# Attention's values times probabilities as three split products, with the transposes in the scores' banks amid the output projection

## The chip, the cores and the metric

The kernel runs on one core of a Trainium2 chip. The metric is the device time of one execution in microseconds; the kernel before takes 1842.34 us, median of three runs (1841.61 to 1843.49). Engines: PE is TensorE (PEld its weight loads), DVE is VectorE, ACT is ScalarE, POOL is GpSimd, SP issues the transfers.

## The reference, cut to what matters

Four layers with a norm and a residual around each: a state-space layer, a gated MLP with integer weights, attention, and a second gated MLP. The input is 4 batches x 256 tokens x 512, all float32. The change lies in attention, which has 32 query heads in 8 groups; each group shares one key and one value head of 128:

```
q = q * cos + rotate_half(q) * sin
scores = einsum('bhqd,bhkd->bhqk', q, k) * scale          # causal mask
attn = softmax(scores)
out  = einsum('bhqk,bhkd->bhqd', attn, v)                 # the product that is changed
return out.reshape(b, 256, 4096) @ Wo.T                   # output projection
```

## The kernel before

The attention phase (`attention_mlp_phase`) works in 32 units, one for each group g (8) and batch b (4), v = 4g + b. A unit has 4 query heads and 256 queries in two halves of 128 (QT = 2). Because of the causal mask the first 128 queries need only the first 128 keys; so a unit has three blocks of transposed probabilities, 128 keys x 512 (4 heads x 128 queries): first half, second half on keys 0, second half on keys 1.

Most matmuls are split: each operand is written as a high part (rounded to float32r by ScalarE) and a low part (the rest, by VectorE or GpSimd), and high x high, high x low and low x high are added. The scores and the product of values and probabilities are plain float32 matmuls; the profile shows such a matmul as two (x2).

PSUM has eight banks of 512 float32 columns: 0 and 1 hold the queries' product (`ps_q`), 2 to 4 the scores (`s0`, `s1`), 5 to 7 are `X[0]`, `X[1]`, `X[2]`. Before the change the three transposes go to `X[2]`, `X[0]`, `X[1]`, are copied to SBUF as `pt`, and the products of values go to `X[2]` and `X[0]`; the output projection of a unit also goes to `X[0]` (t=0) and `X[1]` (t=1).

Each engine has its own queue, written out by hand in a `body(g, b)`, and semaphores order them. TensorE's body for unit v is: `queries` of v+1 (48 split matmuls, L1355); `output` of v-1 (24 split matmuls, L1380 to L1382); `attend` of v (12 transposes, L1389 and L1394, and the float32 products, L1398 to L1402); `scores` of v+1 (L1366, L1368). Meanwhile the next query is made ready: ScalarE's `turn` (L1491, L1492) copies it with its halves exchanged, GpSimd's `sine` (L1631) multiplies that in SBUF, VectorE's `cosine` (L1703) multiplies the unturned one out of PSUM, and `rotate` (L1710) adds the two in SBUF. After the scores VectorE adds the mask and takes maxima (L1715 to L1722), ScalarE takes exponentials (L1500, L1503), and VectorE multiplies by the inverse sums (`probabilities`, L1728 to L1733).

Weights: in b=2 ScalarE splits the next group's query weights and GpSimd makes their low part (L1635); in b=0 the same is done for the output weights (L1515, L1639). `accumulate` (L1739) adds the output projection to `acc` on VectorE.

VectorE's queue before, in one unit:

```
values(v)                  # copy V to vs, L1804
cosine(v + 1)
accumulate(v - 1)          # t = 0, 1; waits for the output projection
copy X[0] to pt            # L1816
rotate(v + 1)
ol = X - oh, t = 0, 1      # L1823
maxima(v + 1); probabilities(v + 1)
```

Of the kernel before, what the change touches and what calls it, by code (L numbers as in the profile page):

```python
# [1237 lines left out]
def attention_mlp_phase(nc, M, place, raw, wqh, wql, K, V, acc, wq, wo, w_mlp, b_mlp, hidden, down, mid,  # L1238
# [12 lines left out]
    flipped, p_kept_act, p_kept_dve, v_here, summed, o_hi, o_lo, o_prod, added = (  # L1251
        sem("flipped"), sem("p_kept_act"), sem("p_kept_dve"), sem("v_here"), sem("summed"), sem("o_hi"), sem("o_lo"),
# [16 lines left out]
    q = place("q", [P, HPG, SEQ])  # L1269
    direct, turned = place("direct", [P, HPG * SEQ]), place("turned", [P, HPG * SEQ])  # L1270
    pa, pb = place("pa", [P, HPG, P]), place("pb", [P, HPG, SEQ])
    pt = place("pt", [P, 3, HALF])
    oh, ol = place("oh", [P, QT, HALF], F32R), place("ol", [P, QT, HALF], F32R)
    vs = place("vs", [P, QT, HD])
# [6 lines left out]
    X = [M.ps[:, 5 + i, :] for i in range(3)]  # L1281
    ps_t = [M.ps[:, i % 2, :] for i in range(TT)]
# [30 lines left out]
    with nc.Block() as block:  # L1313
# [30 lines left out]
        def _(pe):  # L1344
# [26 lines left out]
            def output(g, b):  # L1371
                v = g * BATCH + b
                if b == 0:
                    pe.wait_ge(wo_hi, g + 1)
                    pe.wait_ge(wo_lo, g + 1)
                pe.wait_ge(o_lo, v * 2 + 2)
                for t in range(QT):
                    for h in range(HPG):
                        part = slice(h * P, (h + 1) * P)
                        nc.tensor.matmul(X[t], oh[:, t, part], woh[:, h, :], start=(h == 0), stop=False)  # L1380
                        nc.tensor.matmul(X[t], oh[:, t, part], wol[:, h, :], start=False, stop=False)  # L1381
                        mm = nc.tensor.matmul(X[t], ol[:, t, part], woh[:, h, :], start=False, stop=(h == HPG - 1))  # L1382
                    mm.then_inc(o_prod, 1)

            def attend(g, b):
                v = g * BATCH + b
                pe.wait_ge(normed, v + 1)
                for h in range(HPG):
                    mm = nc.tensor.transpose(X[2][:, h * P:(h + 1) * P], pa[:, h, :], ident)  # L1389
                mm.then_inc(flipped, 1)  # L1390
                for i in range(QT):
                    at_least(pe, added, v * 2 - 1 + i)
                    for h in range(HPG):
                        mm = nc.tensor.transpose(X[i][:, h * P:(h + 1) * P], pb[:, h, i * P:(i + 1) * P], ident)  # L1394
                    mm.then_inc(flipped, 1)
                pe.wait_ge(v_here, v + 1)
                pe.wait_ge(p_kept_act, v * 2 + 1)
                nc.tensor.matmul(X[2], vs[:, 0, :], pt[:, 0, :], start=True, stop=True).then_inc(summed, 1)  # L1398
                pe.wait_ge(p_kept_dve, v + 1)
                nc.tensor.matmul(X[0], vs[:, 0, :], pt[:, 1, :], start=True, stop=False)  # L1400
                pe.wait_ge(p_kept_act, v * 2 + 2)
                nc.tensor.matmul(X[0], vs[:, 1, :], pt[:, 2, :], start=False, stop=True).then_inc(summed, 1)  # L1402
# [37 lines left out]
            def body(g, b):  # L1440
                if more(g, b):
                    queries(*after(g, b))
                if b > 0:
                    output(g, b - 1)
                elif not (isinstance(g, int) and g == 0):
                    output(g - 1, BATCH - 1)
# [9 lines left out]
            output(GROUPS - 1, BATCH - 1)  # L1456
# [29 lines left out]
        def _(act):  # L1486
# [70 lines left out]
            def body(g, b):  # L1557
# [12 lines left out]
                act.wait_ge(flipped, v * 3 + 1)  # L1570
# [7 lines left out]
                for t, x in ((0, X[2]), (1, X[0])):  # L1578
                    act.wait_ge(summed, v * 2 + t + 1)
                    nc.scalar.activation(oh[:, t, :], x, ACT.Copy).then_inc(o_hi, 1)  # L1580
# [498 lines left out]
```

## Time and profile before

| | |
|---|---|
| median of three runs | 1842.34 us (1841.61 to 1843.49) |
| the profiled execution | 1840.51 us |
| its span, first to last instruction | 1838.7 us |
| mean granted TensorE clock | 0.971 of full speed |
| TensorE busy | 1676.4 us, 91% of the span, 8214 matmuls |
| VectorE / ScalarE / GpSimd busy | 1097.3 / 869.0 / 822.2 us |
| HBM traffic | 54 GB/s over the span |

The profile is of one execution. A row of the timeline is one instruction, or several alike after each other (xN): start, duration, engine, line of the kernel, operation, output and input. A matmul's duration is longer than the distance to the next, since they are pipelined; the distance from start to start is what a matmul costs. In brackets stands how long the engine had been idle and what ended that. The attention units run from about 951 us to 1572 us of the span.

### The profile page before, as it was taken

How to read it: one execution, taken by the hardware profiler on the slowest of the kernel's cores; microseconds unless marked ns; L12 is line 12 of the kernel's file. 1: busy time of each engine (PE TensorE's matmuls, PEld its weight loads, DVE VectorE, ACT ScalarE, POOL GpSimd, SP SyncE). 2: the span in 40 equal slices, each digit the busy share in tenths (PEclk: the TensorE clock that was granted, in tenths of full speed). 3: DMA queues.
4: the chain of work that ended last, by engine and by line, in shares of the span. 5: the costliest groups of instructions: out<-in, count | busy, mean ns of one | idle time of the engine just before them, and what ended most of it. 6: DMA issues, size and time to landing. Idle time of an engine off the chain costs nothing. (4 is left out here: it accounts for less than half of the span.)

```text
span 1838.7 us, 24233 instructions
## 1 busy us (share of the span) xinstructions
PE 1676.4 (91%) x8214; PEld 1376.5 (75%) x8214; DVE 1097.3 (60%) x1592; ACT 869.0 (47%) x1761; POOL 822.2 (45%) x416
## 2 busy tenths in 40 slices
PE   5994999999998799898989999999999998799988
PEld 4851788888886688676877778787788786778777
DVE  4326999999995332452915666666666767622232
ACT  2336777777763353333624445454444545433231
POOL 2200999999984362342512232222222323365353
PEclk9997999999999899998999999999999999999989
DMA  3101100011100394001100010000100010144100
GB/s 113 63 1 72 47 35 35 36 34 35 34 0 24 134 355 163 18 1 57 63 23 24 24 47 23 23 23 23 46 23 23 23 58 35 70 142 160 42 18 29
DMA packets 25188, 100.84 MB, mean 55 GB/s; under 512 B 3104, under 2 KB 3360, under 8 KB 22560
## 3 DMA queue, kind: packets, MB, share of 16 engines
q1 hardware_dynamic: 24976, 99.89, 15.1%
q8 instruction: 40, 0.66, 0.1%
q14 instruction: 28, 0.23, 0.0%
q10 hardware_dynamic: 144, 0.07, 0.0%
HBM read 97.72 MB, written 2.23 MB: 54 GB/s over the span
## 5 line engine op out<-in xcount | busy, mean ns | idle before, releaser
L1001 PE MATMUL psum<-scratch_s,res_const 128*128 128x256 f32 x1024 | 250.4, 383 | 4.7 <-DVE scratch_s L960 4.0
L1631 POOL TENSOR_TENSOR stretch_turned<-stretch_turned,res_const 128x1024 f32<-128x1024 f32 x32 | 80.3, 2509 | 386.6 <-ACT stretch_turned L1492 386.6
L1001 PEld LDWEIGHTS psum<-scratch_s,res_const 128*128 128x128 f32 x1024 | 191.8, 190 | 43.0 <-DVE scratch_s L960 18.3
L858 POOL TENSOR_TENSOR scratch_s<-scratch_s,scan_cm 128x1024 f32<-128x1024 f32 x64 | 150.9, 2358 | 27.6 <-DVE scratch_s L944 27.6
L944 DVE TENSOR_TENSOR_SCAN scratch_s<-psum,scratch_s 128x512 f32<-128x512 f32 x128 | 153.4, 1198 | 8.5 <-ACT psum L899 8.5
L1355 PE MATMUL psum<-opnd_xh,query_wqh 128*128 128x256 f32 x512 | 151.5, 296 | 1.9 <-PEq L94 1.9
L846 POOL TENSOR_TENSOR scratch_s<-scan_bm,scratch_s 128x1024 f32<-128x1024 f32 x64 | 150.9, 2359 | 0.1
L1355 PE MATMUL psum<-opnd_xh,query_wql 128*128 128x256 f32 x512 | 145.6, 284 | 0.0
L1355 PE MATMUL psum<-opnd_xl,query_wqh 128*128 128x256 f32 x512 | 145.5, 284 | 0.0
L1500 ACT ACTIVATE stretch_pa<-psum,stretch_nm 128x128 f32<-128x128 f32 x128 | 45.2, 365 | 197.0 <-DVE stretch_nm L1722 197.0
L995 PE MATMUL psum<-scan_diag,scratch_s 128*128 128x256 f32 x512 | 132.9, 383 | 0.5 <-ACT scratch_s L891 0.5
L899 ACT ACTIVATE psum<-ssm_dt,ssm_vec 128x255 f32 (+1 forms) x256 | 110.8, 465 | 11.8 <-DVE scratch_s L944 11.3
L995 PEld LDWEIGHTS psum<-scan_diag,scratch_s 128*128 128x128 f32 x512 | 95.9, 193 | 13.0 <-ACT scratch_s L891 0.9
L1355 PEld LDWEIGHTS psum<-opnd_xh,query_wqh 128*128 128x128 f32 x512 | 99.0, 193 | 3.2 <-issue 2.3
L1380 PE MATMUL psum<-stretch_woh,stretch_oh 128*128 128x512 f32 x256 | 100.3, 392 | 0.5 <-DVE stretch_ol L1823 0.5
L1381 PE MATMUL psum<-stretch_wol,stretch_oh 128*128 128x512 f32 x256 | 100.0, 390 | 0.0
L1382 PE MATMUL psum<-stretch_woh,stretch_ol 128*128 128x512 f32 x256 | 99.9, 390 | 0.0
L1355 PEld LDWEIGHTS psum<-opnd_xl,query_wqh 128*128 128x128 f32 x512 | 98.9, 193 | 0.8
L1355 PEld LDWEIGHTS psum<-opnd_xh,query_wql 128*128 128x128 f32 x512 | 98.7, 193 | 0.0
L235 PE MATMUL psum<-stretch_wh,stretch_hh 128*128 128x512 f32 x176 | 71.1, 404 | 17.2 <-ACT stretch_wh L284 15.5
L960 DVE TENSOR_TENSOR scratch_s<-psum,scan_cm 128x512 f32<-128x512 f32 x128 | 85.2, 665 | 0.0
L950 DVE TENSOR_TENSOR_SCAN psum<-scan_decay,psum 128x512 f32<-128x512 f32 x64 | 78.1, 1221 | 0.0
(269 smaller groups left out, 4322.4 us busy)
## 6 DMA issues: line engine op xcount, KB each, us to landing
mi_dw<-in_dw SPq DMA_DIRECT2D x24, 448.0 KB, 5.7
mi_dm<-in_dm SPq DMA_DIRECT2D x24, 448.0 KB, 6.4
query_raw<-in_w_q SPq DMA_DIRECT2D x8, 1024.0 KB, 4.7
query_raw<-in_w_o SPq DMA_DIRECT2D x8, 1024.0 KB, 4.8
scan_cm<-bc_rows SPq DMA_DIRECT2D x12, 512.0 KB, 4.1
gu_raw<-in_w_gu SPq DMA_DIRECT2D x11, 512.0 KB, 8.0
mlpa_raw<-in_w_mlp SPq DMA_DIRECT2D x7, 768.0 KB, 4.3
mlpa_base<-in_b_mlp SPq DMA_DIRECT2D x7, 768.0 KB, 5.8
```

What stands on the lines that cost most here:

```text
L846: nc.gpsimd.tensor_tensor(by_state(shared[r][h]), bm[:, 4 * h:4 * h + 4, :], u[r].rearrange("p (a t) -> p a t", a=1).broadcast_to((P, 4, S ...
L858: nc.gpsimd.tensor_tensor(shared[r][h], shared[r][h], weights(4 * h, 4), ALU.mult).then_inc(weighted_pool, 1)
L899: ins = nc.scalar.activation(by_state(bank)[:, n, 1:SEQ], flat_dt[:, bass.ds(s * SEQ + 1, SEQ - 1)], ACT.Exp, scale=M.vec[:, bass.ds(s * N ...
L944: nc.vector.tensor_tensor_scan(quarter(r, i), decay_shared[i % 2], quarter(r, i), 0.0, ALU.mult, ALU.add).then_inc(scanned, 1)
L960: nc.vector.tensor_tensor(own[i], state[i], weights(NH + 2 * i, 2), ALU.mult).then_inc(weighted, 1)
L995: mm = nc.tensor.matmul(by_state(state[i])[:, :, t * P:(t + 1) * P], ut[r][:, t * P:(t + 1) * P], diag[:, t, 2 * i:2 * i + 2, :], start=Tr ...
L1001: mm = nc.tensor.matmul(ps_y[r], ident, part[:, n * SEQ:(n + 1) * SEQ], start=False, stop=stop and (n + 1) * SEQ == part.shape[1])
L1355: mm = nc.tensor.matmul(ps_q[:, h * SEQ:(h + 1) * SEQ], w[:, k, h * HD:(h + 1) * HD], x[:, k, b * SEQ:(b + 1) * SEQ], start=(k == 0 and w ...
L1380: nc.tensor.matmul(X[t], oh[:, t, part], woh[:, h, :], start=(h == 0), stop=False)
L1381: nc.tensor.matmul(X[t], oh[:, t, part], wol[:, h, :], start=False, stop=False)
L1382: mm = nc.tensor.matmul(X[t], ol[:, t, part], woh[:, h, :], start=False, stop=(h == HPG - 1))
L1631: nc.gpsimd.tensor_tensor(heads(turned[:, :]), heads(turned[:, :]), over_heads(C_SIN, SEQ), ALU.mult).then_inc(q_sine, 1)
```

## The change

The product of values and probabilities is split like the others. ScalarE writes `vh` (rounded values) and `ph` (rounded probabilities, all three blocks) and VectorE writes `vl` and `pl`, the rests. Nine float32r matmuls take the place of three float32 ones. The transposes go to `turned_p`, banks 2 to 4 of the scores, and stand on TensorE between the first half of the heads of the t=1 output projection of the unit before and its second half (in the last unit after all of it). The projection's input `oh`, `ol` of t=0 shares its memory with `ph`, `pl` block 0; `direct` and `q` share one buffer, and `rotate` works in place. VectorE accumulates t=0 before, t=1 after the subtractions and `rotate`. The start of the diff renames semaphores accordingly.

```diff
@@ -1266,12 +1266,13 @@
     woh, wol = place("woh", [P, HPG, DM], F32R), place("wol", [P, HPG, DM], F32R)
-    q = place("q", [P, HPG, SEQ])
-    direct, turned = place("direct", [P, HPG * SEQ]), place("turned", [P, HPG * SEQ])
+    q, turned = place("q", [P, HPG, SEQ]), place("turned", [P, HPG * SEQ])
+    direct = q[:, :, :].rearrange("p a c -> p (a c)")
     pa, pb = place("pa", [P, HPG, P]), place("pb", [P, HPG, SEQ])
-    pt = place("pt", [P, 3, HALF])
-    oh, ol = place("oh", [P, QT, HALF], F32R), place("ol", [P, QT, HALF], F32R)
-    vs = place("vs", [P, QT, HD])
+    ph, pl = place("ph", [P, 3, HALF], F32R), place("pl", [P, 3, HALF], F32R)
+    o_last = [place(n, [P, HALF], F32R) for n in ("oh", "ol")]
+    oh, ol = (ph[:, 0, :], o_last[0][:, :]), (pl[:, 0, :], o_last[1][:, :])
+    vh, vl = place("vh", [P, QT, HD], F32R), place("vl", [P, QT, HD], F32R)
     mx, nm, sums, inv = (place(n, [P, 8]) for n in ("mx", "nm", "sums", "inv"))
...
@@ -1279,6 +1280,7 @@
     X = [M.ps[:, 5 + i, :] for i in range(3)]
+    turned_p = [M.ps[:, 2 + i, :] for i in range(3)]
     ps_t = [M.ps[:, i % 2, :] for i in range(TT)]
...
@@ -1368,38 +1370,50 @@
 
-            def output(g, b):
+            def output(g, b, t, first=0, end=HPG):
                 v = g * BATCH + b
-                if b == 0:
-                    pe.wait_ge(wo_hi, g + 1)
-                    pe.wait_ge(wo_lo, g + 1)
-                pe.wait_ge(o_lo, v * 2 + 2)
-                for t in range(QT):
-                    for h in range(HPG):
-                        part = slice(h * P, (h + 1) * P)
-                        nc.tensor.matmul(X[t], oh[:, t, part], woh[:, h, :], start=(h == 0), stop=False)
-                        nc.tensor.matmul(X[t], oh[:, t, part], wol[:, h, :], start=False, stop=False)
-                        mm = nc.tensor.matmul(X[t], ol[:, t, part], woh[:, h, :], start=False, stop=(h == HPG - 1))
+                if first == 0 and t == 0:
+                    if b == 0:
+                        pe.wait_ge(wo_hi, g + 1)
+                        pe.wait_ge(wo_lo, g + 1)
+                    pe.wait_ge(o_lo, v * 2 + 2)
+                if first == 0:
+                    at_least(pe, added, v * 2 - 1 + t)
+                for h in range(first, end):
+                    part = slice(h * P, (h + 1) * P)
+                    nc.tensor.matmul(X[t], oh[t][:, part], woh[:, h, :], start=(h == 0), stop=False)
+                    nc.tensor.matmul(X[t], oh[t][:, part], wol[:, h, :], start=False, stop=False)
+                    mm = nc.tensor.matmul(X[t], ol[t][:, part], woh[:, h, :], start=False, stop=(h == HPG - 1))
+                if end == HPG:
                     mm.then_inc(o_prod, 1)
 
-            def attend(g, b):
+            def flips(g, b):
                 v = g * BATCH + b
                 pe.wait_ge(normed, v + 1)
                 for h in range(HPG):
-                    mm = nc.tensor.transpose(X[2][:, h * P:(h + 1) * P], pa[:, h, :], ident)
+                    mm = nc.tensor.transpose(turned_p[0][:, h * P:(h + 1) * P], pa[:, h, :], ident)
                 mm.then_inc(flipped, 1)
                 for i in range(QT):
-                    at_least(pe, added, v * 2 - 1 + i)
                     for h in range(HPG):
-                        mm = nc.tensor.transpose(X[i][:, h * P:(h + 1) * P], pb[:, h, i * P:(i + 1) * P], ident)
+                        mm = nc.tensor.transpose(turned_p[1 + i][:, h * P:(h + 1) * P], pb[:, h, i * P:(i + 1) * P], ident)
                     mm.then_inc(flipped, 1)
-                pe.wait_ge(v_here, v + 1)
-                pe.wait_ge(p_kept_act, v * 2 + 1)
-                nc.tensor.matmul(X[2], vs[:, 0, :], pt[:, 0, :], start=True, stop=True).then_inc(summed, 1)
-                pe.wait_ge(p_kept_dve, v + 1)
-                nc.tensor.matmul(X[0], vs[:, 0, :], pt[:, 1, :], start=True, stop=False)
-                pe.wait_ge(p_kept_act, v * 2 + 2)
-                nc.tensor.matmul(X[0], vs[:, 1, :], pt[:, 2, :], start=False, stop=True).then_inc(summed, 1)
+
+            def attend(g, b):
+                v = g * BATCH + b
+                pe.wait_ge(v_hi, v + 1)
+                pe.wait_ge(v_lo, v + 1)
+                at_least(pe, o_lo, v * 2)
+                for i, (bank, keys) in enumerate(((X[2], 0), (X[0], 0), (X[0], 1))):
+                    pe.wait_ge(p_hi, v * 3 + i + 1)
+                    if i == 1:
+                        at_least(pe, added, v * 2 - 1)
+                    nc.tensor.matmul(bank, vh[:, keys, :], ph[:, i, :], start=(i < 2), stop=False)
+                    nc.tensor.matmul(bank, vl[:, keys, :], ph[:, i, :], start=False, stop=False)
+                pe.wait_ge(p_lo, v * 3 + 1)
+                nc.tensor.matmul(X[2], vh[:, 0, :], pl[:, 0, :], start=False, stop=True).then_inc(summed, 1)
+                pe.wait_ge(p_lo, v * 3 + 3)
+                nc.tensor.matmul(X[0], vh[:, 0, :], pl[:, 1, :], start=False, stop=False)
+                nc.tensor.matmul(X[0], vh[:, 1, :], pl[:, 2, :], start=False, stop=True).then_inc(summed, 1)
 
...
@@ -1440,10 +1454,15 @@
                     queries(*after(g, b))
-                if b > 0:
-                    output(g, b - 1)
-                elif not (isinstance(g, int) and g == 0):
-                    output(g - 1, BATCH - 1)
+                behind = (g, b - 1) if b > 0 else (g - 1, BATCH - 1)
+                any_behind = b > 0 or not (isinstance(g, int) and g == 0)
+                early = HPG if ending(g, b, BATCH - 1) else HPG // 2
+                if any_behind:
+                    output(*behind, 0)
+                    output(*behind, 1, 0, early)
+                flips(g, b)
+                if any_behind and early < HPG:
+                    output(*behind, 1, early)
                 attend(g, b)
...
@@ -1567,17 +1587,17 @@
                 at_least(act, summed, v * 2)
-                act.wait_ge(flipped, v * 3 + 1)
-                nc.scalar.activation(pt[:, 0, :], X[2], ACT.Copy).then_inc(p_kept_act, 1)
-                act.wait_ge(flipped, v * 3 + 3)
-                nc.scalar.activation(pt[:, 2, :], X[1], ACT.Copy).then_inc(p_kept_act, 1)
+                nc.scalar.activation(vh[:, :, :], V[:, QT * b:QT * b + QT, cols(g, HD)], ACT.Copy).then_inc(v_hi, 1)
+                for i in range(3):
+                    act.wait_ge(flipped, v * 3 + i + 1)
+                    nc.scalar.activation(ph[:, i, :], turned_p[i], ACT.Copy).then_inc(p_hi, 1)
                 if ending(g, b, BATCH - 1):
                     x_norm(0)
                     x_norm(1)
                 at_least(act, o_prod, v * QT)
                 for t, x in ((0, X[2]), (1, X[0])):
                     act.wait_ge(summed, v * 2 + t + 1)
-                    nc.scalar.activation(oh[:, t, :], x, ACT.Copy).then_inc(o_hi, 1)
+                    nc.scalar.activation(oh[t], x, ACT.Copy).then_inc(o_hi, 1)
                 if b == 0:
...
@@ -1700,14 +1720,14 @@
                 dve.wait_ge(q_turned, v + 1)
-                nc.vector.tensor_tensor(heads(direct[:, :]), heads(ps_q), over_heads(C_COS, SEQ), ALU.mult).then_inc(q_cosine, 1)
+                nc.vector.tensor_tensor(heads(direct), heads(ps_q), over_heads(C_COS, SEQ), ALU.mult).then_inc(q_cosine, 1)
 
             def rotate(g, b):
                 v = g * BATCH + b
                 dve.wait_ge(q_cosine, v + 1)
                 dve.wait_ge(q_sine, v + 1)
                 at_least(dve, scored, v)
-                nc.vector.tensor_tensor(flat(q), direct[:, :], turned[:, :], ALU.add).then_inc(q_done, 1)
+                nc.vector.tensor_tensor(direct, direct, turned[:, :], ALU.add).then_inc(q_done, 1)
 
...
@@ -1733,10 +1753,9 @@
 
-            def accumulate(v, b):
-                for t in range(QT):
-                    dve.wait_ge(o_prod, v * QT + t + 1)
-                    nc.vector.tensor_tensor(acc[:, QT * b + t, :], X[t], acc[:, QT * b + t, :], ALU.add).then_inc(added, 1)
+            def accumulate(v, b, t):
+                dve.wait_ge(o_prod, v * QT + t + 1)
+                nc.vector.tensor_tensor(acc[:, QT * b + t, :], X[t], acc[:, QT * b + t, :], ALU.add).then_inc(added, 1)
 
...
@@ -1799,28 +1818,31 @@
 
-            def values(g, b, v):
-                at_least(dve, summed, v * 2)
-                nc.vector.tensor_copy(vs[:, :, :], V[:, QT * b:QT * b + QT, cols(g, HD)]).then_inc(v_here, 1)
+            def values_low(g, b, v):
+                dve.wait_ge(v_hi, v + 1)
+                nc.vector.tensor_tensor(vl[:, :, :], V[:, QT * b:QT * b + QT, cols(g, HD)], f32(vh[:, :, :]), ALU.subtract).then_inc(v_lo, 1)
 
             def body(g, b):
                 v = g * BATCH + b
                 last = ending(g, b, BATCH - 1)
-                if not last:
-                    values(g, b, v)
+                behind = not (isinstance(v, int) and v == 0) and not last
                 if more(g, b):
                     cosine(*after(g, b))
-                if not (isinstance(v, int) and v == 0) and not last:
-                    accumulate(v - 1, (b - 1) % BATCH)
-                dve.wait_ge(flipped, v * 3 + 2)
-                nc.vector.tensor_copy(pt[:, 1, :], X[0]).then_inc(p_kept_dve, 1)
+                values_low(g, b, v)
+                if behind:
+                    accumulate(v - 1, (b - 1) % BATCH, 0)
+                for i in range(3):
+                    dve.wait_ge(p_hi, v * 3 + i + 1)
+                    nc.vector.tensor_tensor(pl[:, i, :], turned_p[i], f32(ph[:, i, :]), ALU.subtract).then_inc(p_lo, 1)
                 if last:
                     y_moments_of(1)
                 if more(g, b):
                     rotate(*after(g, b))
+                if behind:
+                    accumulate(v - 1, (b - 1) % BATCH, 1)
                 for t, x in ((0, X[2]), (1, X[0])):
                     dve.wait_ge(o_hi, v * 2 + t + 1)
-                    nc.vector.tensor_tensor(ol[:, t, :], x, f32(oh[:, t, :]), ALU.subtract).then_inc(o_lo, 1)
+                    nc.vector.tensor_tensor(ol[t], x, f32(oh[t]), ALU.subtract).then_inc(o_lo, 1)
                 if more(g, b):
...
```

## Rows read from the trace of the kernel before

**Rows 1.** Busy time in one group's four units (window, then each engine's time, PEclk, DMA).

```profile
1216.54:1291.20 74.66, 72.06 (x427) 60.24 (x426) 49.04 (x88) 34.84 (x92) 19.15 (x6) 1.00 0.08 29
```

**Rows 2.** Timeline of TensorE: the first projection matmul of b=1, 2, 3, 0 and 1.

```profile
1216.54 0.40 PE L1380 MATMUL psum<-stretch_woh,stretch_oh 128*128 128x512 f32 x1
...
1235.18 0.40 PE L1380 MATMUL psum<-stretch_woh,stretch_oh 128*128 128x512 f32 x1
...
1255.37 0.40 PE L1380 MATMUL psum<-stretch_woh,stretch_oh 128*128 128x512 f32 x1
...
1273.24 0.40 PE L1380 MATMUL psum<-stretch_woh,stretch_oh 128*128 128x512 f32 x1
...
1291.10 0.40 PE L1380 MATMUL psum<-stretch_woh,stretch_oh 128*128 128x512 f32 x1
```

**Rows 3.** Waits of TensorE from 980 to 1580 us (total us, times, longest).

```profile
PE psum L1366 <- DVE stretch_q L1710: 16.0, 8, 2.1
...
PE psum L1394 <- DVE acc_acc L1739: 4.1, 8, 0.5
```

**Rows 4.** Timeline of TensorE in the unit b=3 after its projection.

```profile
1260.84 0.60 PE L1389 MATMUL psum<-res_const,stretch_pa 128*128 128x128 f32 x4
...
1262.28 1.02 PE L1398 MATMUL psum<-stretch_pt,stretch_vs 128*128 128x512 f32 x2
...
1264.86 1.05 PE L1366 MATMUL psum<-att_k,stretch_q 128*128 x8
...
1267.29 0.47 PE L1355 MATMUL psum<-opnd_xh,query_wqh 128*128 128x256 f32 x1
```

**Rows 5.** Timeline of VectorE in the same unit.

```profile
1257.74 1.14 DVE L1733 TENSOR_SCALAR stretch_pb<-stretch_pb,stretch_inv 128x256 f32<-128x256 f32 x4
...
1258.99 1.22 DVE L1703 TENSOR_TENSOR stretch_direct<-psum,res_const 128x1024 f32<-128x1024 f32 x1
...
1260.12 0.68 DVE L1739 TENSOR_TENSOR acc_acc<-psum,acc_acc 128x512 f32<-128x512 f32 x1
...
1261.92 0.69 DVE L1816 COPY stretch_pt<-psum 128x512 f32<-128x512 f32 x1 [0.18 <-PE psum L1394]
...
1262.53 1.22 DVE L1710 TENSOR_TENSOR stretch_q<-stretch_direct,stretch_turned 128x1024 f32<-128x1024 f32 x1
```

**Rows 6.** Timeline of ScalarE in the same unit.

```profile
1257.74 1.02 ACT L1492 ACTIVATE stretch_turned<-psum 64x1024 f32<-64x1024 f32 x1
...
1261.48 0.60 ACT L1571 ACTIVATE stretch_pt<-psum 128x512 f32<-128x512 f32 x1 [2.73 <-PE psum L1389]
```

**Rows 7.** Timeline of GpSimd in the same unit.

```profile
1258.83 2.53 POOL L1631 TENSOR_TENSOR stretch_turned<-stretch_turned,res_const 128x1024 f32<-128x1024 f32 x1 [13.16 <-ACT stretch_turned L1492]
```

**Rows 8.** Timelines of GpSimd and VectorE in b=0 and b=2, and L1722 in b=3.

```profile
1210.83 4.61 POOL L1639 TENSOR_TENSOR stretch_wol<-query_raw,stretch_woh 128x2048 fp32r<-128x2048 f32 x1 [6.19 <-ACT stretch_woh L1515]
...
1214.17 1.30 DVE L1722 TENSOR_SCALAR stretch_nm<-stretch_mx 128x8 f32<-128x8 f32 x1
...
1241.15 4.52 POOL L1635 TENSOR_TENSOR query_wql<-query_raw,query_wqh 128x2048 fp32r<-128x2048 f32 x1
...
1242.34 4.41 DVE L1710 TENSOR_TENSOR stretch_q<-stretch_direct,stretch_turned 128x1024 f32<-128x1024 f32 x1
...
1253.01 0.17 DVE L1722 TENSOR_SCALAR stretch_nm<-stretch_mx 128x8 f32<-128x8 f32 x1
```

**Rows 9.** Timeline of all engines at 1542 to 1547 us, last group, b=2.

```profile
1542.03 3.43 POOL L1655 TENSOR_TENSOR mlpb_raw<-mlpb_raw,mlpb_base 128x1536 f32<-128x1536 f32 x1 [1.17 <-DMA mlpb_base<-in_b_mlp]
...
1542.15 4.38 DVE L1710 TENSOR_TENSOR stretch_q<-stretch_direct,stretch_turned 128x1024 f32<-128x1024 f32 x1
...
1545.41 3.48 POOL L1647 TENSOR_TENSOR tok_x<-tok_x,acc_acc 128x512 f32<-128x512 f32 x2
...
1546.59 1.16 PE L1366 MATMUL psum<-att_k,stretch_q 128*128 128x128 f32 x8 [1.87 <-DVE stretch_q L1710]
```

More of the change, by code:

```diff
@@ L1250, in attention_mlp_phase @@
                                                               sem("exped"), sem("inverse"), sem("normed"))
-    flipped, p_kept_act, p_kept_dve, v_here, summed, o_hi, o_lo, o_prod, added = (
-        sem("flipped"), sem("p_kept_act"), sem("p_kept_dve"), sem("v_here"), sem("summed"), sem("o_hi"), sem("o_lo"),
+    flipped, p_hi, p_lo, v_hi, v_lo, summed, o_hi, o_lo, o_prod, added = (
+        sem("flipped"), sem("p_hi"), sem("p_lo"), sem("v_hi"), sem("v_lo"), sem("summed"), sem("o_hi"), sem("o_lo"),
         sem("o_prod"), sem("added"))
@@ L1455, in _ @@
             token_transposes(1)
-            output(GROUPS - 1, BATCH - 1)
+            output(GROUPS - 1, BATCH - 1, 0)
+            output(GROUPS - 1, BATCH - 1, 1)
             weights_split(0)
@@ L1830, in body @@
                 if ending(g, b, 2):
-                    values(g, b + 1, v + 1)
-                    accumulate(v, b)
+                    for t in range(QT):
+                        accumulate(v, b, t)
                     x_moments_of(0)
@@ L1852, in _ @@
             x_moments_of(1)
-            accumulate(U - 1, BATCH - 1)
+            for t in range(QT):
+                accumulate(U - 1, BATCH - 1, t)
             y_moments_of(3)
```

## The prediction

> **What bounds the kernel now.** I read the profile in four steps. First, the busy time over one whole group of four batches [rows 1]: of 74.66 us TensorE is busy 72.06, at a granted clock of 1.00, while VectorE, ScalarE and GpSimd lie at 49, 35 and 19. So TensorE sets the pace of this stage, but busy shares don't say how close the next chain is. Second, the times at which the four units of that group begin their output projection [rows 2]. A unit is one (group, batch). They last 18.64 (b=1), 20.19 (b=2), 17.87 (b=3) and 17.86 us (b=0), 74.56 together. Third, what TensorE waits for [rows 3]: in b=2 for `rotate` (L1710), 16.0 us in all over 8 units; in b=1 for the accumulation (L1739), up to 0.5 us each time. In b=3 and b=0 it waits for nothing. There 17.87 us is pure TensorE work.
>
> Fourth, one such unit, b=3 [rows 2, 4]. Output projection from 1255.37 to 1260.84: 24 products, 5.47 us, so 0.228 each. Twelve transposes to 1262.28: 1.44. Values times probabilities to 1264.86: 2.58. Scores to 1267.29: 2.43. Next queries to 1273.24: 5.95.
>
> Beside it runs the chain that readies the next query [rows 5, 6, 7]: exponentials, `turn` on ScalarE (L1492 ends 1258.76), `sine` on GpSimd (1258.83 to 1261.36), `rotate` on VectorE, which reads the sine (1262.53 to 1263.75). Scores need it by 1264.86, so it has 1.1 us of slack. That slack is the number to watch.
>
> **What is removed.** The fp32 product takes 2.58 us for three products of 512 columns (two passes each). Nine split products at the projection's 0.228 take 2.05: 0.53 us less TensorE work a unit. Where TensorE sets the pace this is worth 0.53 x 31, about 16 us. The copies of values (L1804, 0.2 us of VectorE) and of the probabilities go. The transposes no longer wait for the accumulation, which in b=1 cost 0.54 us and some restart.
>
> **What is moved.** The transposes go ahead of the last six projection products, so they can start at 1255.37 + 18 x 0.228 = 1259.47. The probabilities are ready at 1258.88 (end of L1733) [rows 5], so they don't wait. They write the banks of scores that the exponentials have read. In b=1 I put their wait below 0.3 us. The six products (1.37 us) now lie where the copies out of PSUM start. No DMA is moved.
>
> **What is added.** ScalarE: the high part of the values, 128x256, before the first copy out, and a third copy (0.60) [rows 6]. Turn ends at 1258.76. With 0.60 as an upper bound for a copy half that size, the high values are there by 1259.4. Nothing on ScalarE gets late by this, it then idles. VectorE: the low values (L1739 takes 0.68 us for 512 columns and L1710 1.22 for 1024 [rows 5]; by that slope 256 columns take 0.41), and three subtractions of 0.69, 0.61 from start to start [rows 5], where one copy was. All four stand *ahead of `rotate`* in VectorE's queue. So VectorE has 2 x 0.61 + 0.32 us more to do in front of the instruction that had 1.1 us of slack.
>
> The low values carry one more cost. They subtract one SBUF tensor from another, and at that moment `sine` is running. [Rows 8] show what that does. In b=2 `rotate`, also with both inputs in SBUF, starts at 1242.34 inside a GpSimd operation that ends at 1245.67, and takes 4.41 us in place of 1.22. The small L1722 is likewise held, 1.30 us, until GpSimd's L1639 ends at 1215.44. But operations with one input in PSUM are not held: L1703 and L1739 run 1.22 and 0.68 inside the sine [rows 5, 7]. [Rows 9] show the hand-over: `rotate` is held by L1655 to 1545.46 and ends at 1546.53, that is 1.07 later, 0.15 less than its own 1.22. GpSimd's next operations, already due at 1545.41, take 3.48 for the two and let VectorE in first. The Trainium skill has this as a rule, SBUF — State Buffer, section "Who interferes with whom": a VectorE instruction with two SBUF inputs and a GpSimd instruction that reads SBUF exclude each other for the whole instruction. By it the edit is no gain of 0.53 but a loss; the trace agrees, with 4.41 against 1.22.
>
> **The sum for b=3 and b=0.** VectorE ends the cosine at 1260.0 (0.2 earlier, the copy being gone) and comes to the low values at 1259.93, 1.4 us before the sine ends. Held to 1261.36, ending 1261.36 - 0.15 + 0.41 = 1261.62. Then start to start (an end less 0.08, then steps of 0.61): accumulation t=0 at 1261.54, the subtractions at 1262.15, 1262.76, 1263.37, `rotate` at 1263.98, ending 1265.20. On TensorE: transposes to 1260.91, six products to 1262.28, six high ones to 1263.65, the first low one to 1263.88. The last two wait for the third subtraction (1264.06) and end about 1264.6: no bound. Scores wait for `rotate`. What a restart costs, b=2 of before shows: without a wait its values would have ended at 1235.18 + 5.47 + 1.44 + 2.58 = 1244.67; the unit was 20.19 - 17.87 = 2.32 longer, so scores began in effect at 1246.99, 0.24 after the end of `rotate` (1242.34 + 4.41). The first score matmul itself starts 0.06 after it in [rows 9]; I take 0.24 and keep 0.06 for the range. Scores then begin in effect at 1265.44, not 1264.86: +0.58 a unit in place of -0.53. The pace is then set by exponentials, turn, sine and `rotate`, and TensorE idles 0.7 us.
>
> **b=1.** Before it lost 0.77 us, since L1722 was held 1.13 us (1.30 less its usual 0.17) by GpSimd's L1639 [rows 8]. That operation is tied to the end of the values' product, and the scores now come some 0.8 us later than that, so L1722 is held only about 0.3 us. The chain then gives 17.87 + 0.58 + 0.3 = 18.75 against 18.64: +0.1.
>
> **b=2.** The high values are ready about 1235.18 + 5.6, after ScalarE's query weights, the low ones at GpSimd's boundary near 1241.2. They push L1635 back by 0.41 - 0.13, some 0.3 at most; `rotate`, held by L1635 as before, ends 0.1 to 0.3 later. +0.15.
>
> Per group 0.58 + 0.58 + 0.1 + 0.15 = 1.4 us; eight groups 11.3, less 1 for the first unit (no projection or accumulation in it) and the last (no `rotate`), so about +10.3. At the end two more subtractions stand ahead of the moments of the norm, some 0.4 us. The profiled execution took 1840.5 us around a span of 1838.7; the median is 1842.3. 1842.3 + 10.7 = **1853 us**, +0.6%.
>
> **Rivals.**
> *A, the forecast:* held by the sine, handed over at its end. Chance 0.63. Own range 1846 to 1860: 31 units by 0.2 less for the restart, or by 0.2 more for VectorE's steps.
> *B, the other side, not held:* if the low values run in 0.41 us beside the sine, VectorE is at `rotate` by 1262.70 and done at 1263.92. TensorE then ends the values at 1264.33 and never waits in b=3 and b=0: -0.53 each, -0.3 in b=1, 0 in b=2 (L1635 still holds `rotate`), -1.4 x 8 = 11, so 1831. It decides at one point: if low values end more than 0.58 us before 1261.62, it is a gain. Against it stand the 4.41 us; for it, that the held rows are with longer GpSimd operations and that no row shows `sine` itself holding anything. 0.13.
> *C, the hand-over is lost in b=2:* if L1635 follows the sine without letting VectorE in, the low values end at 1235.18 + 10.8, `rotate` at +14.3 in place of +11.6. 8 x 2.7 = 21 more: 1873. Against it [rows 9]. 0.07.
> *D, the steps nearly cancel:* VectorE's chain is 0.3 to 0.4 us a unit shorter than I add up (steps overlapping the hold, cheaper low values): 1839 to 1846. 0.12.
> *E, TensorE's work alone counts:* -16, and b=1's stall of 0.5 gone, -4: 1822. It needs B and a free `rotate` in b=2 as well, 0.05.
>
> **Numbers.** About 0.2% (3.7 us) is what a measurement of this kernel can tell from no change. Faster: B, E and the lower edge of D, 0.19. Same: most of D and a little of A, 0.12. Slower: 0.69. The likeliest is A, 1853. The range 1830 to 1862 holds A nearly whole, B and D (0.63 + 0.13 + 0.12, less tails), and leaves out C and E.
>
> **What would show it.** Right: the low values' row has a mean near 1.6 us, far over 0.41, in b=1, 3, 0 and near 0.5 in b=2; TensorE waits at the scores for `rotate` in every unit, 0.5 to 0.8 us, and 2.5 in b=2; units of 18.45 us at b=3 and b=0; nine products in about 2.1 us plus a wait. Wrong: low values at 0.4 us in every unit, or a `rotate` that TensorE doesn't wait for in b=3, or a wait for the probabilities at the transposes, which I have at none. If b=2 grows beyond 22 us it is C. A granted clock below 1.00 in this stage would be something that none of my sums hold.

## The result and the profile after

The changed kernel takes 1857.72 us (median of four runs, 1854.76 to 1858.36), the kernel before 1842.16 in the same comparison: ratio 1.008, 95% interval 1.0063 to 1.0098. It is slower by some 15.6 us; the forecast was 1853, +10.7, in a range of 1830 to 1862. In the changed kernel the values' low part is L1823, the three subtractions L1836, `rotate` L1730, the projection's first matmul L1384, the transposes L1394 and L1398, the values' products L1410 to L1416, scores L1368, `sine` L1651 and the low query weights L1655.

First the timeline of TensorE in a unit b=3, which answers to [rows 4] (start, duration, engine, line), and the start of the next unit.

```profile
1266.79 0.40 PE L1384 MATMUL psum<-stretch_woh,stretch_ph 128*128 128x512 f32 x1
...
1270.90 0.60 PE L1394 MATMUL psum<-res_const,stretch_pa 128*128 128x128 f32 x4
...
1272.13 0.48 PE L1384 MATMUL psum<-stretch_woh,stretch_oh 128*128 128x512 f32 x1
...
1273.61 0.40 PE L1410 MATMUL psum<-stretch_ph,stretch_vh 128*128 128x512 f32 x1
...
1275.40 0.50 PE L1415 MATMUL psum<-stretch_pl,stretch_vh 128*128 128x512 f32 x1
1275.75 0.39 PE L1416 MATMUL psum<-stretch_pl,stretch_vh 128*128 128x512 f32 x1
1276.62 1.15 PE L1368 MATMUL psum<-att_k,stretch_q 128*128 x8 [0.48 <-DVE stretch_q L1730]
...
1285.09 0.40 PE L1384 MATMUL psum<-stretch_woh,stretch_ph 128*128 128x512 f32 x1
```

The unit takes 18.30 us, where [rows 2] have 17.87. The nine products run from 1273.61 to about 1275.98, 2.37 with a short wait before L1415; then TensorE waits for `rotate`. The timelines of VectorE and of GpSimd in the same unit say why.

```profile
1270.22 1.22 DVE L1723 TENSOR_TENSOR stretch_q<-psum,res_const 128x1024 f32<-128x1024 f32 x1
1271.36 1.60 DVE L1823 TENSOR_TENSOR stretch_vl<-att_v,stretch_vh 128x256 fp32r<-128x256 f32 x1
1272.88 0.68 DVE L1758 TENSOR_TENSOR acc_acc<-psum,acc_acc 128x512 f32<-128x512 f32 x1
1273.48 1.87 DVE L1836 TENSOR_TENSOR stretch_pl<-psum,stretch_ph 128x512 fp32r<-128x512 f32 x3
1275.28 1.21 DVE L1730 TENSOR_TENSOR stretch_q<-stretch_q,stretch_turned 128x1024 f32<-128x1024 f32 x1
```

```profile
1270.26 2.41 POOL L1651 TENSOR_TENSOR stretch_turned<-stretch_turned,res_const 128x1024 f32<-128x1024 f32 x1 [14.86 <-ACT stretch_turned L1512]
```

The low values start inside the sine and end 0.29 us after it (1272.96 against 1272.67): 1.60 us for an instruction that takes 0.42 elsewhere. Everything to `rotate` is pushed back by that. Now b=2, VectorE and then GpSimd.

```profile
1250.53 0.43 DVE L1823 TENSOR_TENSOR stretch_vl<-att_v,stretch_vh 128x256 fp32r<-128x256 f32 x1 [1.14 <-ACT stretch_vh L1590]
...
1253.27 3.22 DVE L1730 TENSOR_TENSOR stretch_q<-stretch_q,stretch_turned 128x1024 f32<-128x1024 f32 x1
```

```profile
1248.21 2.41 POOL L1651 TENSOR_TENSOR stretch_turned<-stretch_turned,res_const 128x1024 f32<-128x1024 f32 x1 [15.90 <-ACT stretch_turned L1512]
1250.57 4.83 POOL L1655 TENSOR_TENSOR query_wql<-query_raw,query_wqh 128x2048 fp32r<-128x2048 f32 x1
```

Here VectorE got in between the two GpSimd operations, and L1655 took 4.83 in place of 4.52 [rows 8]: the hand-over went as in [rows 9]. TensorE's waits from 980 to 1600 us (total, times, longest) answer to [rows 3].

```profile
PE psum L1368 <- DVE stretch_q L1730: 29.8, 30, 2.5
PE psum L1394 <- DVE stretch_pb L1753: 7.7, 2, 4.5
...
PE psum L1415 <- DVE stretch_pl L1836: 2.3, 9, 0.3
```

Thirty waits for `rotate`, where before there were eight. What I had not seen coming is in the busy time by stretch. The first two rows are the time from the first score matmul to the next projection in two b=2 units, the last two are those whole units (window, busy time of PE, PEld, DVE, ACT, POOL, then PEclk, DMA share, GB/s).

```profile
1256.63:1266.79 10.16, 10.16 (x64) 9.46 (x65) 4.95 (x8) 2.02 (x11) 0.00 (x0) 0.83 0.24 94
1333.92:1342.39 8.47, 8.47 (x64) 8.26 (x65) 4.93 (x8) 2.03 (x11) 0.00 (x0) 1.00 0.26 109
1244.73:1266.79 22.06, 19.48 (x111) 16.67 (x110) 14.33 (x24) 10.26 (x26) 7.20 (x2) 0.92 0.14 48
1322.03:1342.39 20.36, 17.78 (x111) 15.47 (x110) 14.31 (x24) 10.26 (x26) 7.18 (x2) 1.00 0.15 52
```

The same matmuls take 10.16 us in one unit and 8.47 in another, 1.69 more, because the granted clock fell from 2.4 GHz to 1.2 for a time after the wait. The wait ahead of them was 2.50 us in the long unit and 2.49 in the other, so its length doesn't tell the two apart. In the profiled run five of seven b=2 units were long (21.5 to 22.1 us), in the kernel before one (1309.75 to 1331.56, 21.8).

The last group's b=2 has the same fall, after a wait of 1.93 us; in the kernel before, the clock is 1.00 from 1547 to 1553 us, behind its wait of 1.87 [rows 9].

```profile
1561.81 2.08 PE L1368 MATMUL psum<-att_k,stretch_q 128*128 128x128 f32 x8 [1.93 <-DVE stretch_q L1730]
1562.50:1568.00 5.50, 5.50 (x24) 4.82 (x24) 2.85 (x5) 0.00 (x0) 3.92 (x3) 0.79 0.00 0
```

From the first score matmul to the next projection it is 3.96 us, where the kernel before has 2.53 (1546.59 to 1549.12).

The account of the two profiled runs, 1858.36 less 1840.51 = 17.85 us. I add the seven units of each kind from the first matmuls of their projections: b=1 +0.1, b=2 +7.4, b=3 +2.3, b=0 +2.7, together 12.6. Ahead of the first such point lie 2.6 (1.1 of it before attention begins, where nothing was changed), behind the last 2.6, of which 1.43 is the fall just shown. The falls behind the waits of b=2 cost 9.2 us in the changed kernel (six, of 1.3 to 1.7 each) and 1.6 in the kernel before (one). So about 7.5 of the 17.85 us are the clock, 1.1 lie ahead of attention, and some 9 are left for the rest.

### The profile page after: what moved, and what is told of

Its sections match the earlier page's. It is cut to its first block and busy times, and to the rows that moved or that the text cites. A ratio compares the mean times of both kernels' runs of the same rounds, so it can differ in the third digit from the quotient of the medians.

```text
span 1856.5 us, 24771 instructions
## 1 busy us (share of the span) xinstructions
PE 1680.3 (91%) x8310; PEld 1399.1 (75%) x8310; DVE 1146.2 (62%) x1656; ACT 893.3 (48%) x1825; POOL 817.5 (44%) x416
## 5 line engine op out<-in xcount | busy, mean ns | idle before, releaser
L1651 POOL TENSOR_TENSOR stretch_turned<-stretch_turned,res_const 128x1024 f32<-128x1024 f32 x32 | 76.8, 2400 | 401.9 <-ACT stretch_turned L1512 401.9
L950 DVE TENSOR_TENSOR_SCAN psum<-scratch_s,psum 128x512 f32<-128x512 f32 x64 | 78.0, 1219 | 0.0
L899 ACT ACTIVATE scan_decay<-ssm_dt,ssm_vec 128x255 f32 (+1 forms) x128 | 57.9, 499 | 41.4 <-DVE psum L950 41.4
L1368 PE MATMUL psum<-att_k,stretch_q 128*128 (+1 forms) x256 | 41.1, 309 | 35.7 <-DVE stretch_q L1730 35.7
```

The source lines that it names most:

```text
L899: ins = nc.scalar.activation(by_state(bank)[:, n, 1:SEQ], flat_dt[:, bass.ds(s * SEQ + 1, SEQ - 1)], ACT.Exp, scale=M.vec[:, bass.ds(s * N ...
L950: nc.vector.tensor_tensor_scan(state[i], decay_own[i % 2], state[i], 0.0, ALU.mult, ALU.add).then_inc(scanned, 1)
L1651: nc.gpsimd.tensor_tensor(heads(turned[:, :]), heads(turned[:, :]), over_heads(C_SIN, SEQ), ALU.mult).then_inc(q_sine, 1)
```

## The experiments

**1. The low values without the hold.**

```diff
-  tensor_tensor(vl, V[..., cols(g, HD)], f32(vh), subtract)      # values_low
+  tensor_tensor(vl, M.ps[:, 0, 0:QT * HD]..., f32(vh), subtract)
```

> The changed kernel, but the low values are computed from a PSUM bank (the queries' product, 256 columns) less vh, not from V less vh: same size, same place in VectorE's queue, same waits, only one input in SBUF. So the low values are not those of V. Theory (the hold): the instruction takes about 0.4 us beside the sine, rotate ends some 1.2 us earlier, TensorE sets the pace again in b=3 and b=0: units of 17.35 us (5.95 + 5.47 + 1.44 + 2.05 + 2.43) in place of 18.30, b=1 about 18.3; b=2 stays at 20.1 to 20.4 since L1655 still holds rotate; total about 1840 us. Rival (it is the three subtractions and the low values as plain VectorE work, the hold only overlaps them): units stay at 18.1 to 18.3, total 1855.

1835.74 us against 1840.52, ratio 0.9968 (0.9956 to 0.9981). The row of the low values (min/median/max ns):

```profile
L1823 DVE TENSOR_TENSOR stretch_vl<-psum,stretch_vh x32: 414/415/426, 983.1 to 1556.7; 128x256 fp32r<-128x256 f32 x32
```

In the changed kernel the same row reads:

```profile
L1823 DVE TENSOR_TENSOR stretch_vl<-att_v,stretch_vh x32: 415/1580/1602, 981.1 to 1576.0; 128x256 fp32r<-128x256 f32 x32
```

Units of 17.25 us in b=3 and b=0, 18.27 in b=1. One input moved out of SBUF turns the loss into a gain. The low values are then wrong ones, so this kernel computes another result; the amount of work, its place and its waits are the same. The total was 4 us below what I expected.

**2. Less work for TensorE.**

```diff
-  nc.tensor.matmul(bank, vl[:, keys, :], ph[:, i, :], start=False, stop=False)
```

> The changed kernel without the three products of vl with ph (L1411): 0.68 us less of TensorE work in every unit, all waits and all other engines' work as they are; that part of the result is left out. Theory (VectorE's rotate sets the pace): units unchanged at 18.3 in b=3 and b=0, TensorE's wait for rotate grows from 0.5 to about 1.1 us, total within 4 us of the changed kernel's 1857.7, perhaps above it if the longer idle lets the granted clock fall more often. Rival (TensorE's work still sets the pace): 0.68 x 31 = 21 us less, about 1837.

1863.47 us, ratio 1.0121 (1.0102 to 1.014): 0.68 us less work in every unit (one of the three parts of the product is left out) and the kernel is slower still than the changed one, by more than the 4 us that I had allowed. Its waits of TensorE:

```profile
PE psum L1368 <- DVE stretch_q L1729: 29.7, 30, 2.5
PE psum L1414 <- DVE stretch_pl L1835: 19.4, 30, 0.7
```

Units b=3 and b=0 stay at 17.9 to 18.3 us. My guess that the wait for `rotate` would grow was wrong in its place: the idle time appears ahead of the last two products, up to 0.7 us each time, and all seven b=2 units are long, 21.8 to 23.3 us. The long wait is as long as in the changed kernel, with 0.7 us more idle time shortly ahead of it. That the added idle time brought the falls is the likeliest reading; one profiled execution doesn't prove it.

**3. The values split early.**

```diff
@@ ScalarE's body @@
-                nc.scalar.activation(vh[:, :, :], V[:, QT * b:QT * b + QT, cols(g, HD)], ACT.Copy).then_inc(v_hi, 1)
                 for i in range(3):
...
                     nc.scalar.activation(oh[t], x, ACT.Copy).then_inc(o_hi, 1)
+                if more(g, b):
+                    values_high(*after(g, b))
@@ VectorE's body @@
                     cosine(*after(g, b))
-                values_low(g, b, v)
...
                     maxima(*after(g, b))
+                    values_low(*after(g, b), v + 1)
```

> The changed kernel with the split of the values moved out of the way: ScalarE makes vh of the next unit right after the copies of oh, VectorE makes vl right after the maxima, where it idles 3.5 us for the exponentials. Same work, nothing left out. Theory (the hold by the sine is the loss): low values at 0.4 us or held only by L1659 in b=0, where VectorE idles anyway; rotate ends 1.6 us earlier, units of 17.35 in b=3 and b=0, 18.3 in b=1, 20.1 in b=2, so 1.9 us less a group than before's 74.56: 1842 - 12 = about 1830, with 5 us more if the clock falls in b=2. Rival (three subtractions ahead of rotate are enough for a loss): 0.4 us less a unit than the changed kernel, about 1846.

1835.88 us, ratio 0.9969 (0.9957 to 0.9982), within 0.2 us of experiment 1 and with the whole computation. Units: 17.25 in b=3 and b=0, 18.27 in b=1, 20.1 in b=2 with the full clock and 21.8 in four of seven. Its total is 6 us above my 1830. Four falls of the clock at 1.7 us, three more than in the kernel before, account for most of that.

**4. The long wait filled.**

```diff
                 attend(g, b)
+                if b == 2:
+                    pe.wait_ge(q_turned, g * BATCH + b + 2)
+                    pe.wait_ge(q_cosine, g * BATCH + b + 2)
+                    for i in range(9):
+                        nc.tensor.matmul(M.ps[:, 0, :], vh[:, 0, :], ph[:, 2, :], start=True, stop=True)
```

> The changed kernel with nine more products of 512 columns (2.05 us, into a bank of queries that is free) on TensorE in b=2, between the values' product and the wait for rotate, which lasts 2.5 us. Their result is overwritten. Theory (in b=2 the granted clock falls to half for 3.4 us after the 2.5 us idle, 1.7 us lost in five of eight groups): no half-clock stretch in b=2, those units at 20.4, not 22.0; total about 1849. Rival (the falls are not due to that idle): still about five units of 22 us, total 1857 or, as the added work costs time, more.

1849.69 us (1849.27 to 1850.2), 8 us less than the changed kernel with more work on TensorE. (The two were measured against the kernel before at different times; by these ratios, 1.0045 and 1.008, it is 6.4.) A b=2 unit and its filled wait:

```profile
1241.75:1262.16 20.41, 19.84 (x121) 17.17 (x119) 14.35 (x24) 10.27 (x26) 7.23 (x2) 1.00 0.15 51
```

```profile
1250.99 2.21 PE L1471 MATMUL psum<-stretch_ph,stretch_vh 128*128 128x512 f32 x9
1253.69 1.15 PE L1368 MATMUL psum<-att_k,stretch_q 128*128 x8 [0.48 <-DVE stretch_q L1735]
```

All seven units take 20.14 to 20.42 us, at a clock of 1.00. So the falls come from this idle time, and they cost the changed kernel 6 to 8 us. As the kernel before has one of them too, not all of this belongs to the 15.6 us: the account above, 7.5 of 17.85 in the profiled executions, makes it somewhat under half.

**5. GpSimd waits for `rotate` in b=2.** On top of experiment 3:

```diff
                     nc.vector.tensor_tensor(pl[:, i, :], turned_p[i], ...)
+                    if i == 0 and more(g, b):
+                        rotate(*after(g, b))
...
-                if more(g, b):
-                    rotate(*after(g, b))
...
                 if b == 2 and not (isinstance(g, int) and g == GROUPS - 1):
+                    pool.wait_ge(q_done, g * BATCH + b + 2)
                     query_weights(g + 1)
```

> e3_early_values, with two more moves. VectorE's rotate stands behind the first of the three subtractions, not the third; and in b=2 GpSimd waits for that rotate before it makes the low query weights (L1655), so that rotate isn't held by it. Nothing left out. Theory (in b=2 the loss is this hold, plus the granted clock that falls after the idle it causes): rotate ends 7.2 us after the projection's start, the low weights are ready 0.5 us after TensorE wants them, b=2 takes about 17.9 us in place of 20.1 to 21.8, no half-clock stretch; total 1836 - 7 x 3.1, about 1815. Rival (GpSimd's 4.5 us, now 1.3 us later, come late by more than they held, since the queries of the next group wait for them): b=2 at 20 or more, total 1832 to 1840.

1820.22 us (1818.87 to 1826.75), ratio 0.9894 (0.9868 to 0.9919). GpSimd in a unit b=2:

```profile
1232.26 2.44 POOL L1656 TENSOR_TENSOR stretch_turned<-stretch_turned,res_const 128x1024 f32<-128x1024 f32 x1 [14.97 <-ACT stretch_turned L1512]
1236.54 4.55 POOL L1660 TENSOR_TENSOR query_wql<-query_raw,query_wqh 128x2048 fp32r<-128x2048 f32 x1 [1.84 <-DVE stretch_q L1736]
```

b=2 takes 18.48 us, not the 17.9 expected, but with the clock at 1.00 in the unit; TensorE waits at most 0.4 us for the low weights. b=1 rose to 18.81, b=3 and b=0 to 17.4: with `rotate` ahead of two subtractions the last products wait for them (L1415, up to 0.4 us in b=1). The total is 5 us above the 1815 expected.

**6. The maxima scaled on ScalarE.** On top of experiment 5:

```diff
@@ maxima, VectorE @@
-                dve.wait_ge(maxed, v * 2 + 2)
-                nc.vector.tensor_scalar(nm[:, :], mx[:, :], -SCALE, None, ALU.mult).then_inc(neg_max, 1)
@@ exps, ScalarE, ahead of the exponentials @@
+                act.wait_ge(maxed, v * 2 + 2)
+                nc.scalar.activation(nm[:, :], mx[:, :], ACT.Copy, scale=-SCALE).then_inc(neg_max, 1)
```

> e5_gpsimd_waits, and the small scaling of the maxima (128x8, before L1722 on VectorE, held up to 1.3 us by GpSimd's low output weights in b=0) is done by ScalarE. Nothing left out. Theory (b=1 loses 1.0 us to this hold alone, 18.27 against 17.25): b=1 at 17.3, about 8 us less than e5_gpsimd_waits. Rival (b=1 waits for other work of VectorE, or ScalarE's operation costs as much in every unit): within 2 us of e5_gpsimd_waits.

1819.0 us (1815.34 to 1823.18), ratio 0.9872 (0.985 to 0.9895). The mechanism holds, b=1 goes from 18.81 to 17.42 us; the total moved by 1 us, not 8, which is less than the spread of either kernel's executions. Here two lie at 1815.34 and 1816.04 us and two at 1821.96 and 1823.18, and the profiled one is the slowest. In it the stretch behind the last b=1 unit is 6 us longer than in experiment 5. The timelines of the last group's b=2 show how that began, VectorE and then GpSimd:

```profile
1520.04 4.24 DVE L1738 TENSOR_TENSOR stretch_q<-stretch_q,stretch_turned 128x1024 f32<-128x1024 f32 x1
```

```profile
1519.73 3.47 POOL L1682 TENSOR_TENSOR mlpb_raw<-mlpb_raw,mlpb_base 128x1536 f32<-128x1536 f32 x1 [0.82 <-DMA mlpb_base<-in_b_mlp]
```

In experiment 5 `rotate` started 0.11 us ahead of this operation, here 0.31 behind it, and was held by it. TensorE then waited 3.8 us for the subtraction behind it (L1415). The last b=1 unit is 1.6 us longer as well; experiment 9 says why.

**7. One small copy moved into the sine, in the kernel before.**

```diff
-                if not last:
-                    values(g, b, v)
                 if more(g, b):
                     cosine(*after(g, b))
+                if not last:
+                    values(g, b, v)
```

> The kernel before, with one line moved: the copy of the values (L1804, 0.29 us, SBUF to SBUF) stands behind the cosine, so that VectorE comes to it inside the sine. Nothing left out or added. Theory (the hold by the sine alone is costly where TensorE waits for VectorE behind it): the copy takes about 1.5 us, the accumulation and with it TensorE's transposes come 0.9 to 1.1 us late, units of 19.0 in b=3 and b=0, 19.9 in b=1, b=2 nearly as before; total about 1842 + 8 x 3.5 = 1870. Rival (a 0.29 us copy costs the same wherever it stands): 1842, same.

1866.79 us, ratio 1.0141 (1.012 to 1.0162): a moved line costs 25 us.

```profile
L1804 DVE COPY stretch_vs<-att_v x32: 284/1466/1504, 979.4 to 1578.1; 128x256 f32 x24, 128x256 f32<-128x256 f32 x8
```

The copy takes 1.47 us in the median; b=3 and b=0 take 18.71 us (19.0 expected), b=1 19.8, or 21.5 where the clock falls. That it does in four of seven b=1 units, behind a wait of 1.72 us for the accumulation:

```profile
1233.87 1.26 PE L1394 MATMUL psum<-res_const,stretch_pb 128*128 128x128 f32 x8 [1.72 <-DVE acc_acc L1739]
1233.00:1240.00 7.00, 6.13 (x21) 3.41 (x22) 3.92 (x6) 1.76 (x3) 0.06 (x1) 0.76 0.00 0
```

So about 5 of these 25 us are the clock, three falls of 1.7 more than the kernel before has.

**8. The transposes without their cover.** On top of experiment 3:

```diff
-                early = HPG if ending(g, b, BATCH - 1) else HPG // 2
+                early = HPG
```

> e3_early_values with the transposes behind the whole output projection, as before the change: the last six products (1.37 us) no longer lie between the transposes and the values' product. Nothing left out. Theory (the move gives VectorE and ScalarE time to copy and subtract): the third subtraction ends 8.6 us and rotate 9.8 us after the projection's start, TensorE is through with the values' product at 9.1, so it waits 0.8 us and restarts: b=3 and b=0 at 18.2 in place of 17.25, b=2 unchanged, total about 1836 + 0.9 x 16 + some in b=1, 1850 to 1856. Rival (the move doesn't matter once the values are split early): within 2 us of 1836.

1848.15 us, ratio 1.0039 (1.0025 to 1.0053), 2 us below the 1850 to 1856 expected. b=3 and b=0 take 18.37 us in place of 17.25: TensorE waits for `rotate` in every unit again (27.9 us in 30 waits). So the change's own move is worth 1.1 us in each such unit.

**9. The last group's order.** On top of experiment 6, `pool.wait_ge(q_done, U)` ahead of the weights' difference in the last group's b=2.

> e6_scale_on_scalar with one more wait: in the last group's b=2 GpSimd begins the weights' difference (L1655 of before, 3.5 us) only after the last rotate. Nothing left out. Theory (in e6_scale_on_scalar that difference started 0.3 us before rotate and held it for 3.0 us, TensorE idled 3.8 us and the granted clock fell; in e5_gpsimd_waits rotate came first): rotate at 1.2 us in every unit, no wait of 3.8 us, 3 to 6 us less than e6_scale_on_scalar, about 1814. Rival (the tail is bound by the weights' chain on GpSimd, so the later difference costs what the hold did): 1817 to 1821.

1814.82 us (1814.47 to 1815.6), ratio to the kernel before 0.9861 (0.9844 to 0.9877). `rotate` in all 32 units (min/median/max ns):

```profile
L1739 DVE TENSOR_TENSOR stretch_q<-stretch_q,stretch_turned x32: 1209/1216/1228, 964.2 to 1517.7; 128x1024 f32<-128x1024 f32 x32
```

No wait of 3.8 us is left. This version beats both kernels, the changed one by some 40 us. Its last b=1 still takes 20.36 us, where experiment 5 has 18.73. TensorE waits 2.5 us for the probabilities there, whose multiplications are held twice: L1758 by a weights' difference, and L1760 then by the sine (VectorE, then GpSimd):

```profile
1491.96 2.06 DVE L1758 TENSOR_SCALAR stretch_pa<-stretch_pa,stretch_inv 128x128 f32<-128x128 f32 x4
1493.94 3.25 DVE L1760 TENSOR_SCALAR stretch_pb<-stretch_pb,stretch_inv 128x256 f32<-128x256 f32 x4
```

```profile
1489.65 3.70 POOL L1682 TENSOR_TENSOR mlpa_raw<-mlpa_raw,mlpa_base 128x1536 f32<-128x1536 f32 x1
1493.85 2.41 POOL L1658 TENSOR_TENSOR stretch_turned<-stretch_turned,res_const 128x1024 f32<-128x1024 f32 x1 [0.49 <-ACT stretch_turned L1512]
```

In experiment 5 they take 0.87 and 1.13 us. The same hold is back at another place; no run here removes it.

## Why the prediction was right, and where its sum was off

The mechanism is the one forecast: the low values are held by the sine, and `rotate`, not TensorE's work, sets the pace. That the total lies only 5 us above the forecast is in part luck, since a missing term, the clock, is larger than that and the rest of the sum was too high.

*TensorE's work* (0.53 us a unit): right as a saving that exists and isn't collected. Experiment 1 collects it, 17.87 to 17.25, 0.62; the nine products take 2.06 us in experiment 3, 2.05 forecast.

*The hold by the sine:* right, and shown rather than argued by experiments 1 and 7. The forecast put the end of the low values 6.25 us after the projection's start, measured 1272.96 - 1266.79 = 6.17; `rotate`'s end 9.83, measured 9.70. The sine itself was 0.12 us shorter (2.41 against 2.53 [rows 7]) now that no copy (L1804) stands at its start; in experiment 7, where the copy comes later, it is 2.41 too. What the restart costs behind `rotate`'s end was forecast at 0.24, and the unit of 18.30 gives 0.22. Units of b=3 and b=0: +0.58 forecast, +0.43 measured in the middle groups and +0.15 to +0.31 in five units near the two ends. Rival B's unit of 17.34 us is nearly that of experiments 1 and 3 (17.25), so the point from which it decides was the right one.

*The three subtractions ahead of `rotate`:* no loss by themselves. In experiments 1 and 3 they stand there and TensorE waits for `rotate` in b=2 alone, in experiment 1 also in one more unit, as long as six projection products cover them (experiment 8).

*b=1:* +0.1 forecast, 0.0 measured. The small L1722 (now L1742) was held less, as argued: it takes at most 0.77 us, in the middle groups 0.53, in place of 1.30.

*b=2:* +0.15 forecast; +0.18 where the clock stays at 1.00 (20.36 against 20.18). Rival C, the lost hand-over, didn't occur.

*The clock:* this term was missing. The prediction said that a granted clock below 1.00 was in none of its sums. Before, one wait of b=2 in eight was followed by a fall; after, six in eight. The difference is about 7.5 us, and filling the wait gave back 6 to 8 (experiment 4). Without it some 8 to 9 us are left, less than the 10.7 forecast: the sum was 0.15 us a unit too high in b=3 and b=0, more near the two ends, and came near the total because the clock made up for it. This count is of one execution of each kernel. The others' mean clocks (0.968 to 0.971 before, 0.963 to 0.965 after) suggest that the number of falls varies between executions.

*The ends:* 0.4 forecast behind the last unit, 2.6 measured between the profiled runs. 1.43 of it is the fall behind the last b=2; from the last transposes to the last projection it is 0.24 more (7.88 us against 7.64), and the remaining 0.9 lies in the phases behind attention and stays open. At the start the first unit takes 1.5 us more (952.36 to 995.69 against 951.29 to 993.08), where the sum had nothing: no projection lies there between the transposes and the products, and TensorE waits 0.73 us at L1410.

## What to carry to other kernels

Before an instruction is added, ask which queue it stands in, what on another engine runs at that moment, and what waits behind it: here 0.4 us of work with both inputs in SBUF cost more than the matmuls it made possible saved, and the same work some 7 us earlier cost nothing that can be measured. An engine that is 96% busy doesn't set the pace if a chain beside it has 1.1 us of slack and gets 1.3 more (`rotate` ends 9.70 us after the projection's start, before 8.38); count the chain to its end. And a wait of TensorE has a second price, the clock after it: fill it or shorten it, and look at single units, since a mean hides that some are 1.7 us longer. After each repair look again at what now meets what: in experiments 6 and 9 the hold came back at other places.

## What the runs showed of the hardware that I had not expected

TensorE's granted clock fell to half behind idle times of 1.7 to 2.7 us, and not each time. In the profiled execution of each kernel, in seven groups:

| kernel | TensorE's wait in the unit | units after which the clock was halved |
|---|---|---|
| before, b=2 | 1.77 to 2.06 us | 1 of 7 |
| experiment 8, b=2 | 1.94 to 2.26 | 3 of 7 |
| experiment 1, b=2 | 2.30 to 2.41 | 4 of 7 |
| changed, b=2 | 2.40 to 2.50 | 5 of 7 |
| experiment 3, b=2 | 2.42 to 2.66 | 4 of 7 |
| experiment 2, b=2 | 2.39 to 2.49, and 0.7 shortly before | 7 of 7 |
| experiment 7, b=1 | 1.58 to 1.73 | 4 of 7 |
| experiment 7, b=2 | 1.03 to 1.13 | 0 of 7 |
| experiment 4, b=2, filled | 0.39 to 0.49 | 0 of 7 |

Each fall cost 1.3 to 1.7 us; in experiment 2 the units grew by up to 2.9. The length of the one wait isn't all that counts: 1.7 us were enough four times in experiment 7, and 2.06 only once before. What decides in the single case stays open. The Trainium skill speaks of this in TensorE: Matmul & The Clock Gate, section "Why this matters for your kernels", which wants no idle gaps between bursts of matmuls beyond a length that is greater than every wait in this table. Here gaps of 1.7 to 2.7 us were enough in many units, so the measurement decides.

VectorE and GpSimd exclude each other in both directions, operation by operation. It doesn't take two inputs in SBUF: the copy L1804 has one, and it was held (1.47 us in place of 0.29). Every held instruction shown here reads SBUF alone; L1703 and L1739 [rows 5], with one input in PSUM, ran their usual time inside the sine. The other way round, the sine ran 0.12 us longer when a VectorE copy stood at its start, and whether `rotate` came 0.11 us before or 0.31 us behind a GpSimd operation decided over 3.0 us of VectorE's time (4.24 in place of 1.22). An order between two engines that no semaphore fixes can turn when something else gets faster (experiment 6).
